# Quantised FFN, attention, FFN on one core: the order inside each FFN round of VectorE, GpSimd and ScalarE

## What is computed

```python
x = x + 0.5 * ffn(layernorm(x))
x = x + attention(layernorm(x))
x = x + 0.5 * ffn(layernorm(x))

def fp4_quant_dequant(x):            # blocks of 16 along the last dim
    scale = max(max(abs(block)) / 6.0, 1e-12)
    idx = searchsorted(_MID, abs(block / scale))
    return _GRID[idx] * sign(block) * scale

gate = fp4_linear(x, w_gate)         # both operands quantised; 256 -> 704
y = fp4_linear(x, w_up)
h = silu(gate) * y
out = fp4_linear(h, w_down)          # h quantised again; 704 -> 256
```

## Time and profile before

| | |
|---|---|
| median of 3 runs (range) | 1028.17 us (1027.7 to 1029.42) |
| the profiled execution | 1027.9 us, span 1026.1 us |
| mean granted TensorE clock | 0.986 of full |
| PE busy | 971.1 us, 95% |
| VectorE (DVE) busy | 736.6 us, 72% |
| ScalarE (ACT) busy | 586.6 us, 57% |
| GpSimd (POOL) busy | 344.7 us, 34% |

### The profile page before, as it was taken

One profiled execution on the slowest core, in us unless ns is written; L12 is line 12 of the kernel. 1 busy time (PEld: TensorE's weight loads), 2 busy tenths in 40 slices (PEclk: granted clock), 3 DMA queues, 4 the chain that ended last, 5 costly groups with the idle time before them and its releaser, 6 DMA issues.

```text
span 1026.1 us, 16471 instructions
## 1 busy us (share of the span) xinstructions
PE 971.1 (95%) x5647; PEld 843.7 (82%) x5647; DVE 736.6 (72%) x1298; ACT 586.6 (57%) x1209; POOL 344.7 (34%) x473
## 2 busy tenths in 40 slices
PE   3799999999998999999999899999998999999997
PEld 2578888888887888888888688888877888888886
DVE  7888988888755555555566555555566898988996
ACT  5767878777645444444455344555455656565553
POOL 3446666665404000000011200000002556556552
PEclk9999999999999999999999999999998999999999
DMA  9000000000000000000000000000000000000001
GB/s 317 19 1 1 1 1 1 1 1 1 1 1 1 1 0 0 0 0 0 0 1 1 0 1 0 0 0 0 0 0 1 1 22 21 21 21 22 15 7 42
DMA packets 11526, 13.48 MB, mean 13 GB/s; under 512 B 848, under 2 KB 10576, under 8 KB 11472
## 3 DMA queue, kind: packets, MB, share of 16 engines
q1 hardware_dynamic: 11472, 12.79, 3.8%
HBM read 8.59 MB, written 4.19 MB: 12 GB/s over the span
## 4 chain that ended last, share of the span: by engine, by line
PE 80%; DVE 11%; POOL 3%; ACT 3%; issue 2%; DMA 0%; SPq 0%; DVEq 0%; POOLq 0%; ACTq 0%
PE bank L1357 19%; PE bank L1547 18%; PE bank L1573 11%; PE bank_b L1366 8%; PE bank L1258 6%; PE bank L1575 6%; PE bank L1262 5%; POOL zq L468 3%; PE bank L1522 2%; DVE amax L628 2%; DVE grid L656 2%; PE bank L1387 2%; DVE rounded L650 1%; DVE z L617 1%; PE bank_b L1538 1%
## 5 line engine op out<-in xcount | busy, mean ns | idle before, releaser
L468 POOL TENSOR_TENSOR zq<-grid,s_neg 128x64 f32<-128x64 f32 (+2 forms) x188 | 178.1, 972 | 61.8 <-DVE grid L656 57.2
L1573 PE MATMUL bank<-v_hl,pT_hi 128*128 128x512 f32 x512 | 185.1, 403 | 0.0
L1197 ACT ACTIVATE pT_hi<-bank 128x512 fp32r<-128x512 f32 x127 | 75.6, 598 | 160.8 <-PE bank L1258 160.7
L1357 PE MATMUL bank<-w_hi,T_hi 128*128 128x512 f32 (+1 forms) x384 | 151.2, 394 | 1.7 <-DVE z L617 1.0
L1357 PE MATMUL bank<-w_lo,T_hi 128*128 128x512 f32 (+1 forms) x384 | 145.5, 379 | 0.0
L1357 PE MATMUL bank<-w_hi,T_lo 128*128 128x512 f32 (+1 forms) x384 | 145.3, 378 | 0.0
L1575 PE MATMUL bank<-v_hl,pT_lo 128*128 128x256 f32 x512 | 143.9, 281 | 0.0
L372 POOL TENSOR_TENSOR var<-var,eps_all (+1 forms) x32 | 6.2, 195 | 369.4 <-ACT st_junk L993 369.4
L833 DVE TENSOR_TENSOR pT_lo<-bank,pT_hi 128x512 fp32r<-128x512 f32 x127 | 87.6, 691 | 49.2 <-ACT pT_hi L1197 49.2
L1547 PE MATMUL bank<-k_hi,q_hi 128*128 128x512 f32 x256 | 110.2, 430 | 7.8 <-DVE q_lo L785 7.8
L1573 PEld LDWEIGHTS bank<-v_hl,pT_hi 128*128 128x128 f32 x512 | 96.3, 188 | 22.1
(11 more groups left out here) (185 smaller groups left out, 2051.3 us busy)
## 6 DMA issues: line engine op xcount, KB each, us to landing
out<-x SPq DMA_DIRECT2D x7, 512.0 KB, 2.9
x<-in_L_attn_hidden_states SPq DMA_DIRECT2D x3, 1024.0 KB, 13.9
x<-in_L_attn_hidden_states SPq DMA_DIRECT2D x2, 512.0 KB, 8.0
wraw<-in_L_ffn_w_down SPq DMA_DIRECT2D x1, 704.0 KB, 8.6
wraw<-in_L_ffn_w_gate SPq DMA_DIRECT2D x1, 640.0 KB, 4.5
wraw<-in_L_ffn_w_up SPq DMA_DIRECT2D x1, 640.0 KB, 6.7
wq_s<-in_L_attn_Wq SPq DMA_DIRECT2D x1, 512.0 KB, 8.5
wk_s<-in_L_attn_Wk SPq DMA_DIRECT2D x1, 512.0 KB, 9.2
```

The costliest lines, as they stand in the source:

```text
L468: last = nc.gpsimd.tensor_tensor(out=blocks(zq[:, to:to + hi - lo]), in0=blocks(grid[:, lo:hi]), in1=spread(s_neg[:, par, lo // BLOCK:hi / ...
L1197: nc.scalar.activation(pT_hi[:, 4 * ch:4 * ch + 4, :].rearrange("p a q -> p (a q)"), transposed(b, i, ch), ACT.Copy).then_inc(phi_done, 1)
L1357: last = nc.tensor.matmul(gu[:, lo:hi], lhsT=T[:, par, HK + kd, :], rhs=w[:, kd, lo:hi], start=n == 0, stop=n == len(terms) - 1)
L1573: nc.tensor.matmul(bank_a[:], lhsT=pT_hi[:, t, :], rhs=v_hl[:, t, :], start=t == 0, stop=False)
```

## The change

Within a round: VectorE does to_grid(c + 1) first, then scales(c + 2). (In the written-out rounds below c = -3 it did so before.) GpSimd does quantised(c + 1) ahead of scaled_x(c + 2). ScalarE's `absolute` moves from the top of round c + 1 to the end of round c, behind the silu and ahead of normalise, with one call more before each loop.

In the head of the first FFN, a one-element silu right at the start (`warm`) brings the table load forward, silu_gate(0) goes ahead of normalise(3) and the input statistics of tiles 4 to 7 (x_means(1), x_variances(1)), and the chain of tile -3 between and around them. In round 0 PE does the first 6 matmuls of gate_up(3) ahead of weight_lower(G1 + 2).

```diff
@@ gpsimd, step(c, par)
+                    if chain(c + 1) and c + 1 < NT - 1:
+                        quantised(c + 1, 1 - par)
                     if hidden(c + 2) and ahead(c + 2):
                         scaled_x(c + 2)
-                    if chain(c + 1) and c + 1 < NT - 1:
-                        quantised(c + 1, 1 - par)
@@ vector, blocks_of(c, par)
-                    if c < -3 and chain(c + 1):
+                    if chain(c + 1):
                         to_grid(c + 1)
                     if chain(c + 2):
                         scales(c + 2, par)
-                    if c >= -3 and chain(c + 1):
-                        to_grid(c + 1)
                     if f and hidden(c) and not late(c):
                         lower_first(c, par)
@@ scalar, start and step(c, par)
+            act.wait_ge(half_set, 1)
...
-                    if chain(c + 1):
-                        absolute(c + 1)
...
                     if c >= 0 and hidden(c + 3):
                         silu_gate(c + 3)
+                    if chain(c + 2):
+                        absolute(c + 2)
                     if c + 7 < NT:
                         normalise(c + 7)
@@ scalar, head of the first FFN
+            nc.scalar.activation(warm[:], mhalf[:, 0:1], ACT.Silu)
             weight_abs(0)
...
             weight_abs(4)
+            silu_gate(0)
+            normalise(3)
+            absolute(-2)
+            chain_upper(-3, 1)
             x_means(1)
-            normalise(3)
+            chain_rest(-3, 1)
+            woT_out(0)
             x_variances(1)
-            absolute(-2)
-            silu_gate(0)
-            chain_upper(-3, 1)
-            woT_out(0)
-            chain_rest(-3, 1)
             woT_out(1)
             weight_abs(5)
             normalise(4)
+            absolute(-1)
             ffn_rounds(step, -2)
@@ tensor, round 0 of the first FFN
-                    if extra and c == 0:
-                        weight_lower(G1 + 2)
                     if gated and c >= 0:
                         pe.wait_ge(gu_read, NT * f + c + 3)
                         gate_up(1 - par, ((0, 512),))
+                    if extra and c == 0:
+                        weight_lower(G1 + 2)
```

More of the change, by code:

```diff
@@ L89, in macaron_kernel @@
         st_junk = sb("st_junk", [P, 2, D])
+        warm = sb("warm", [P, 1])
         rstd = sb("rstd", [P, NT])
```

## The result

The changed kernel takes **1056.38 us** (median of 4 runs, 1054.99 to 1057.98), the kernel before 1027.93 (4 runs, 1025.92 to 1029.42): ratio 1.0271, 95% interval 1.0256 to 1.0286. It is slower by 28 us; the forecast was 1053.8. The profiled execution has a span of 1054.1 us against 1026.1.

A forecast was written before the change was run, and what follows sets the result against it. A loop over one round (rounding, zq, held s_up, y, |y|, rounding) was taken to bound both FFNs; +11.3 us in the first and +14.6 in the second on the profiled 1027.9 gave 1053.8 us, range 1033 to 1063.

The forecast's parts named there:

- Rival 1: Both FFNs: s_up gets its turn in time, PE stays the bound and the kernel gets faster, 1019 us; chance 0.12.
- The floor of 7.27: First FFN, steady rounds: PE's own work of 7.04 plus one 512-column product, about 7.27 us a round.
- s_up held to the end of the 704 piece: Steady rounds: s_up, ready 3.38 us after the rounding's start, waits for GpSimd's 704-column piece until 4.33, ends at 4.40.
- The length of the rounds: Steady rounds, from one rounding to the next: 7.65 us in the first FFN, 7.68 in the second.
- The second hold of the first FFN: First FFN rounds: VectorE's y starts first and holds GpSimd's x part of y, which ends at 6.49 us.
- Rounds with statistics: First FFN: in 5 of the rounds counted, statistics ahead of VectorE's product add 1.01 us each.
- First FFN, +11.3: First FFN: 25 rounds of 7.65 plus 5 x 1.01 give +11.6; head and PE's new place make -0.3 together.
- Head: Head of the first FFN: 5.32 us PE wait goes, zq(-2) wait of about 2 comes; early silu worth about 0.
- The 1.7 for TensorE's reordered round 0: Head of the first FFN: gate_up(3) runs on ahead of the weights in PE's round 0, -1.7 us.
- Second FFN, +14.6: Second FFN: 26 rounds of 7.68 against 187.15 us give +12.5, plus 2.1 for PE's place.
- TensorE's place: PE's rounds open later relative to the rounding, costing 2.1 us once in the second FFN, 1.4 in the first.
- Rival 3: Steady rounds: PE, idle 0.6 us in each, gets a lower clock; one more us a round gives 1105; chance 0.02.

The follow-up runs named there:

- e1: The changed kernel with the block maxima (amax) written to free PSUM columns, so s_up and s_neg read one SBUF tile instead of two: 1019.3 us.
- e4: The changed kernel with GpSimd's old order, the x part of y ahead of zq: 1039.6 us.
- e5: The changed kernel with VectorE's old order alone, scales ahead of rounding and grid: 1130.9 us.
- e9: The changed kernel with VectorE's T_lo subtraction taken ahead of the maxima and scales in the second FFN: 1053.9 us.
- e7: The changed kernel with ScalarE's old head (no early silu or warm-up), TensorE's reordered round 0 kept: 1057.0 us.
- e10: e1 with ScalarE's old head, TensorE's round 0 staying reordered: 1018.9 us.
- e3: The kernel before with only the change's head: early silu, its order of the head and TensorE's reordered round 0: 1024.7 us.
- e2: The changed kernel with GpSimd's 704-column piece of zq cut into two of 352: 1049.2 us.

## Why the prediction was right

**What bounds.** Right: a loop over one round of rounding, zq, held s_up, reciprocal, y, |y|. e1 shows that the hold is the cause, e4 and e5 that it goes wherever zq and the scales are not side by side, e9 that the loop and not VectorE's own work is the bound. Rival 1 (TensorE stays the bound, 1019 us) stands for the case in which s_up is not held, and e1 took 1019.3. That agreement is partly luck: rival 1 put the two stretches at -3 and -4 us, and in e1 they are -5.9 and -0.2 (178.84 and 186.96). The floor of 7.27 that the prediction gave TensorE in the first FFN was too high, it runs at 7.15 there; in the second the loop stays the bound.

One reading of the rows was incomplete: before the change zq did not run mostly beside operations that read PSUM. Its 704 piece met VectorE's y and took 2.04 for 1.39 us, so the exclusion stood in every round already, on an engine that could bear it.

**s_up held to the end of the 704 piece.** Predicted 3.38 to 4.40 after the rounding's start; it is 3.44 to 4.48. The small s_neg stood ahead of the reciprocal, which ended at 5.17 (predicted 5.10). The 64 piece held it, 0.33 for 0.21; it did not slip in ahead. The prediction took the exclusion from the Trainium skill, "SBUF — State Buffer", section "Who interferes with whom". The trace agrees: s_up ended 0.08 after the recorded end of the 704 piece, as in the earlier trace rows. It also weighed the handover figure of that page's section "A bandwidth-pool intuition that's wrong (but worth ruling out)", as an estimate of 0.27 us more a round and 1068 us. The page measured that figure on a DMA kept waiting by VectorE, and for VectorE behind GpSimd the trace shows an earlier end than it would give, 0.08 instead of 0.34 after the piece.

**The length of the rounds.** 7.65 and 7.68 predicted, 7.76 in both. 0.07 of the missing 0.11 and 0.08 is in the rounding: grid starts 1.19 after it instead of 1.12. The rounding took 1.09 in the earlier trace rows and takes 1.16 here. In e5, where it stands behind the reciprocal again, it takes 1.09 to 1.10; in e4, behind the product like here, 1.16 without a wait. So its place decides; why, no run shows. The second hold of the first FFN, GpSimd's y behind VectorE's, is there in every round:

```profile
119.68 1.33 POOL L453 TENSOR_TENSOR y<-z,s_inv 128x256 f32<-128x256 f32 x1 [0.59 <-DVE s_inv L641]
```

It ends 6.57 after its rounding's start (114.44); 6.49 was predicted.

**Rounds with statistics.** Mis-sized: +1.01 predicted, +0.52 measured. In the earlier trace rows y's start to the product took 2.73 us; now it takes 2.27 (119.64 to 121.91), because one tiny operation between them took 0.62 before and 0.17 after:

```profile
117.48 0.62 DVE L543 TENSOR_SCALAR nmean<-mv 128x4 f32<-128x4 f32 x1
121.76 0.17 DVE L544 TENSOR_SCALAR nmean<-mv 128x4 f32<-128x4 f32 x1
```

Before, it ended with GpSimd's 704 piece (118.10; the three pieces end at 118.33, the 704 one at about 118.08); after, GpSimd stands idle. I had carried a duration over into a round where its neighbour is another. That is 0.46 of the 0.49 missing. Five such rounds gave 2.5 us less, the pitch 25 x 0.11 = 2.8 more. Two errors cancel, which is luck: 196.8 measured against 196.3. That the stage came out is no proof of its parts.

**First FFN, +11.3.** The stretch gives +12.1 (predicted +11.6); to the last rounding of the stage (290.71 against 279.46) it is +11.25.

**Head.** Early silu worth about 0: right for these rounds (e7, e10). The 5.32 us wait is gone, and the new wait for zq of tile -2 is there, at 1.36 instead of about 2. The 1.7 for TensorE's reordered round 0 no run tests alone; round 0 opens to round 1 in 8.00 us instead of 8.55. On the old rounds (e3) the whole head gives 3.5 us, twice my 1.7.

**Second FFN, +14.6.** Mis-sized, +16.6 in the stretch: 26 x 0.08 = 2.1 from the pitch. TensorE's place was put at 2.1 and is 1.8: the first round takes 9.53 (809.87 to 819.40), 1.77 over the pitch. One more round takes 8.07 (842.66 to 850.73), 0.3 that I had not foreseen; it is there in e1 too (7.57). The 2.0 us of this stage are most of the difference between 1053.8 and the profiled 1055.9.

**TensorE idle 0.7 us a round.** The granted TensorE clock is 1.00 in both stretches, as in the earlier trace rows. Rival 3 is out. Attention, unchanged in the code, took 0.5 less; what follows the last rounding 0.7 more.

## What to carry to other kernels

Before an order is changed, list for each pair of engines what will run beside what, and where the operands of both lie: here one small operation became almost five times as long (1.04 for 0.22 us), because its two inputs lay in SBUF beside a 1.4 us instruction of GpSimd. Then follow what is queued behind the operation that waits. The remedy was an operand in PSUM (37 us), not shorter pieces (7 us), where the hold moves on to the next operation with two tiles in SBUF, nor another place in the queue (2.5 us), where the next such pair took up what was won. Orders on three engines that were made for each other can't be judged one at a time: of the parts undone alone one gave 17 us back, one lost 13, one lost 74.

## What was not expected of the hardware

- The scales and y, VectorE's operations with two tiles in SBUF, were held wherever these traces show them starting inside one of GpSimd's multiplications of 256 columns or more, however small they were: s_up of 60 columns took 1.04 us for 0.22, s_neg 0.82 for 0.21 (e2), y 1.29 for 0.88 to 0.98 (e1). It also works the other way: GpSimd's 256 columns took 1.33 for 0.62 behind VectorE's 704, in e9 and in every round of the first FFN of the change. A GpSimd instruction of one column held nothing that can be seen: in the change y of 256 columns (788.29) took 0.43 inside a 0.55 us `rstd` (788.18).
- Not held beside zq were the reduction (one SBUF input, 1.14 and 1.15), the reciprocal (0.52 in e1) and T_lo (one PSUM input, 0.68 in e9, 0.62 where it stands behind zq). One operation with a single SBUF input does look held, L543 of 4 columns (0.62 for 0.17); no run settled it.
- While it holds s_up GpSimd itself isn't slower: zq's three pieces take 2.23 us with s_up waiting and without (the change, e1). Beside VectorE's y of 704 columns they take 2.87 (e5): there VectorE is the one that holds.
